# A mixture-of-experts stage whose fifth group of rows is halved and worked ahead of the fourth

## The reference

```
probs = softmax(x @ gate_w); w, sel = top_k(probs, 8); w = w / sum(w)
# each expert gets the rows (tokens) that chose it, at most C = 2048
g = xg @ w_gate[e]; u = xg @ w_up[e]
y = (silu(g) * u) @ w_down[e]
out = zeros.at[t_slot].add(w_slot[:, None] * y)
x = x + out
```

## Time and profile before

| | |
|---|---|
| median of 3 runs | 2238.33 us |
| the profiled execution | 2235.58 us |
| its span | 2233.8 us |
| mean granted TensorE clock over the span | 0.976 |
| TensorE matmul busy | 2041.8 us (91%) |
| VectorE / ScalarE / GpSimd busy | 1682.9 / 1149.9 / 1541.2 us |
| first transpose of the experts' stage | 1172.8 us |

### The profile page before, as it was taken

One profiled execution on the slowest core, in us unless ns is written; L12 is line 12 of the kernel. 1 busy time (PEld: TensorE's weight loads), 2 busy tenths in 40 slices (PEclk: granted clock), 3 DMA queues, 4 the chain that ended last, 5 costly groups with the idle time before them and its releaser, 6 DMA issues. The chain is left out here.

```text
span 2233.8 us, 67151 instructions
## 1 busy us (share of the span) xinstructions
PE 2041.8 (91%) x22647; PEld 1497.9 (67%) x22712; DVE 1682.9 (75%) x3294; ACT 1149.9 (51%) x2826; POOL 1541.2 (69%) x1776
## 2 busy tenths in 40 slices
PE   1899999999999999999509999999999999999997
PEld 1576667666666676666306777777777777777775
DVE  6688999999999999997426677676776677666664
ACT  3355555565555556555314455555555555555553
POOL 7336667666766666666667777777777777777774
PEclk9999999999999999999859999999999999999998
DMA  3101100110111001001016888887788878987875
GB/s 104 39 26 40 39 28 28 38 34 28 33 38 33 28 33 38 33 24 45 21 34 154 174 181 164 187 181 174 168 173 180 184 175 169 186 185 161 180 158 87
DMA packets 141452, 222.72 MB, mean 100 GB/s; under 512 B 32944, under 2 KB 65840, under 8 KB 141360
## 3 DMA queue, kind: packets, MB, share of 16 engines
q0 software_dynamic: 74752, 144.02, 32.8%
q1 hardware_dynamic: 62000, 69.24, 10.1%
q10 hardware_dynamic: 4608, 8.39, 1.0%
HBM read 136.34 MB, written 96.73 MB: 104 GB/s over the span
## 5 line engine op out<-in xcount | busy, mean ns | idle before, releaser
L2151 POOL DMA_INDIRECT out_dram<-y,m_add x300 | 499.1, 1664 | 173.8 <-POOLq L2159 116.8
L2277 PE MATMUL ps<-xh,wh 128*128 128x256 f16 x1752 | 399.9, 273 | 6.9 <-PEq L2289 6.9
L2278 PE MATMUL ps<-xh,wl 128*128 128x256 f16 x1752 | 399.9, 273 | 0.0
L2143 POOL DMA_INDIRECT xg<-z_scratch,slot_t x292 | 295.3, 1011 | 96.8 <-issue 86.2
L630 POOL DMA_INDIRECT slot_scratch<-pair,slots x256 | 277.5, 1084 | 68.8 <-issue 47.6
L2354 ACT ACTIVATE y<-ps,wts_now 128x512 f32<-128x512 f32 x294 | 185.4, 682 | 141.3 <-ACTq L2353 141.2
L2282 PE MATMUL ps<-xl,wh 128*128 128x256 f16 x1752 | 239.6, 273 | 0.0
L2428 DVE SCALAR_TENSOR_TENSOR hx<-ps,s 64x256 f16<-64x256 f32 x146 | 62.2, 426 | 219.3 <-DVEq L2451 218.6
L2277 PEld LDWEIGHTS ps<-xh,wh 128*128 128x128 f16 x1752 | 171.7, 98 | 48.7 <-issue 15.4
L2370 ACT ACTIVATE xh<-ps 128x512 f16<-128x512 f32 x146 | 87.2, 597 | 224.4 <-ACTq L2369 224.4
L2278 PEld LDWEIGHTS ps<-xh,wl 128*128 128x128 f16 x1752 | 171.8, 98 | 33.7 <-issue 0.3
(11 more groups left out here) (341 smaller groups left out, 5108.9 us busy)
## 6 DMA issues: line engine op xcount, KB each, us to landing
wst<-in_L_ffn_w_gate_dram SPq DMA_DIRECT2D x32, 384.0 KB
wst<-in_L_ffn_w_up_dram SPq DMA_DIRECT2D x32, 384.0 KB
xt<-in_x_dram SPq DMA_DIRECT2D x32, 256.0 KB
ct<-in_ctx_dram SPq DMA_DIRECT2D x32, 256.0 KB, 2.6
out_dram<-x SPq DMA_DIRECT2D x32, 256.0 KB, 2.1
z_scratch<-zn ACTq DMA_DIRECT2D x32, 256.0 KB
wdst<-in_L_ffn_w_down_dram SPq DMA_DIRECT2D x32, 256.0 KB
out_dram<-y,m_add POOLq DMA_INDIRECT x300, 5.2
```

The lines of the kernel that those rows point to most:

```text
L2143: pool.indirect_dma_start(out=xg[b][:, h, :], out_offset=None, in_=z_d[:, :], in_offset=bass.IndirectOffsetOnAxis(ap=rows(h), axis=0)).the ...
L2151: pool.indirect_dma_start(out=acc_d[:, :], out_offset=bass.IndirectOffsetOnAxis(ap=m_add[:, k, h:h + 1], axis=0), in_=y[:, k, h, :], in_of ...
L2277: pe.matmul(ps[:, dst, 0:GROUP], wh[:, j, k, c0:c0 + P], xh[:, k, :], start=(k == 0), stop=False)
L2278: pe.matmul(ps[:, dst, 0:GROUP], wl[:, j, k, c0:c0 + P], xh[:, k, :], start=False, stop=False)
```

## The change

Rows 1024 to 1151 of an expert become a half group of one part (128 rows), in buffer 4, on all engines. It is worked after group 2 and ahead of group 3 (rows 768 to 1023). If an expert has more than 1152 rows, rows 1152 to 1279 follow behind group 3 as a group of their own with 256 row slots, whose second part is not used: its row numbers are set to spare ones that lie outside the output (`spare_rows`, `note_first`). Group 5 and later ones follow as before. Group 2 has no branch any more. ScalarE's loop is written out. The counts of landed scatters are kept for each part of a y buffer instead of for each buffer.

GpSimd's order for an expert with more than 1024 rows is now: gather group 2; scatter the last group of the expert before; gather the half group; wait for the scatters of earlier experts; scatter group 0; gather group 3; scatter group 1; gather group 0 of the next expert; scatter group 2; gather group 1 of the next expert; scatter the half group; and with more than 1152 rows: gather the rows from 1152 on; scatter group 3; and with more than 1280: gather group 5; scatter the group of the rows from 1152 on.

The diff, cut to its core:

```diff
@@ constants, GpSimd @@
+                    pool.iota(spare_rows[:, :].bitcast(mybir.dt.int32), pattern=[[P, 1]], base=TOK, channel_multiplier=1).then_inc(pool_step, 1)
@@ block2 @@
+            HALF_FROM = 4 * GROUP
+            HALF_TO = HALF_FROM + P
@@ GpSimd @@
+                def add_half(k):
+                    pool.reg_add(n_added[k][0], n_added[k][0], 16)
+                    pool.wait_ge(wy_ready[0], 1)
+                    pool.sem_inc(wy_ready[0], -1)
+                    scatter(k, 0)
+                def gather_half(e):
+                    gather(4, lambda h: slot_t[:, e * (CAP // P) + HALF_FROM // P, 0:1], 1)
+                def gather_rest(e):
+                    gather(4, lambda h: slot_t[:, e * (CAP // P) + HALF_TO // P + h, 0:1])
                 def expert(e):
                     n = pool.value_load(counts[0:1, e:e + 1], min_val=1, max_val=CAP)
+                    more = e + 1 < ne
+                    gather_group(e, 2, 2)
+                    add_rows(2)
+                    with pool.If(n > HALF_FROM):
+                        gather_half(e)
+                    with pool.If(n <= HALF_FROM):
+                        with pool.If(n > 3 * GROUP):
+                            gather_group(e, 3, 3)
+                    earlier_experts_added()
+                    add_rows(1)
+                    if more:
+                        with pool.If(n <= HALF_FROM):
+                            gather_group(e + 1, 0, 0)
+                    with pool.If(n > HALF_FROM):
                         gather_group(e, 3, 3)
+                    add_rows(0)
+                    with pool.If(n <= HALF_FROM):
                         if more:
                             gather_group(e + 1, 1, 1)
+                        with pool.If(n > 3 * GROUP):
+                            add_rows(1)
+                    with pool.If(n > HALF_FROM):
+                        if more:
+                            gather_group(e + 1, 0, 0)
+                        add_rows(1)
+                        if more:
+                            gather_group(e + 1, 1, 1)
+                        add_half(0)
+                        with pool.If(n > HALF_TO):
+                            gather_rest(e)
+                            add_rows(1)
+                            with pool.If(n > USUAL * GROUP):
+                                gather_group(e, USUAL, 2)
+                                add_rows(0)
+                            for g in range(USUAL + 1, NGRP):
+                                with pool.If(n > g * GROUP):
+                                    gather_group(e, g, 3)
+                                    add_rows(1)
@@ TensorE: turn, down and gate_up take the number of parts @@
-                    def group(g, b):
-                        turn(b)
-                        down(j, b)
-                        gate_up(j)
-                    group(1, 1)
+                    def group(b, parts=2, parts_before=2):
+                        turn(b, parts)
+                        down(j, b, parts_before)
+                        gate_up(j, parts)
+                    group(1)
                     n = count_of(pe, e)
-                    written_out_groups(pe, n, group)
+                    group(2)
+                    with pe.If(n > HALF_FROM):
+                        group(4, 1)
+                        group(3, 2, 1)
+                    with pe.If(n <= HALF_FROM):
+                        with pe.If(n > 3 * GROUP):
+                            group(3)
+                    with pe.If(n > HALF_TO):
+                        group(4)
+                        with pe.If(n > USUAL * GROUP):
+                            group(2)
+                            with pe.Fori(USUAL + 1, NGRP) as g:
+                                with pe.If(n > g * GROUP):
+                                    group(3)
@@ ScalarE @@
+                def weigh_half(k):
+                    all_scattered(k)
+                    act.activation(m_add[:, k, :], rows_now[:, :], ACT.Copy)
+                    act.reg_add(n_added[k][0], n_added[k][0], 16)
+                    act.wait_ge(y_ps, 1)
+                    act.sem_inc(y_ps, -1)
+                    act.activation(y[:, k, 0, :], ps[:, 5, :], ACT.Copy, scale=wts_now[:, 0:1]).then_inc(act_step, 1)
...
+                def note_first(col):
+                    act.activation(rows_now[:, 0:1], slot_t[:, bass.ds(col, 1), 0], ACT.Copy)
+                    act.activation(rows_now[:, 1:2], spare_rows[:, :], ACT.Copy)
+                    act.activation(wts_now[:, 0:1], slot_t[:, bass.ds(col, 1), 1].bitcast(F32), ACT.Copy).then_inc(act_step, 1)
...
+                    group(c0 + 4, 0)
+                    with act.If(n > HALF_FROM):
+                        group(c0 + 8, 1, parts=1)
+                        group(c0 + 6, 0, weigh=weigh_half)
+                    with act.If(n <= HALF_FROM):
+                        with act.If(n > 3 * GROUP):
+                            group(c0 + 6, 1)
+                    with act.If(n > HALF_TO):
+                        group(c0 + 9, 1, note=note_first)
...
```

More of the change, by code:

```diff
@@ L2245, in turn @@
                             k = 2 * bank + n
-                            for h in range(2):
+                            for h in range(parts):
                                 c0 = n * GROUP + h * P
@@ L2249, in turn, with down @@
                         m.then_inc(signal, 1)
-                def down(j, b=None):
+                def down(j, b=None, parts=2):
                     pe.wait_ge(hx2_ready, 2)
                     pe.sem_inc(hx2_ready, -2)
-                    for h in range(2):
+                    for h in range(parts):
                         o, t = ps[:, 5 + h, :], slice(h * P, h * P + P)
@@ L2350, in weigh @@
                     act.activation(m_add[:, k, :], rows_now[:, :], ACT.Copy)
+                    for h in range(2):
+                        act.reg_add(n_added[k][h], n_added[k][h], 16)
                     for h in range(2):
@@ L2432, in gated, with group @@
                     dve.tensor_tensor(low, full, hi, ALU.subtract).then_inc(low_signal, 1)
-                def group(split=None, look=None):
+                def group(split=None, look=None, parts=2):
+                    t = slice(0, parts * P)
+                    rows = [ps[:, bank, :].rearrange("p (k t) -> p k t", k=2)[:, :, t] for bank in range(2)]
                     dve.wait_ge(rows_ps_dve, 1)
                     dve.sem_inc(rows_ps_dve, -1)
-                    dve.tensor_copy(xh[:, 2:4, :], ps[:, 1, :].rearrange("p (k t) -> p k t", k=2)).then_inc(xh_high_k_pe, 1)
+                    dve.tensor_copy(xh[:, 2:4, t], rows[1]).then_inc(xh_high_k_pe, 1)
                     dve.wait_ge(xh_low_k, 1)
@@ L2462, in expert @@
                     n = group((lambda: split_low_down(1 - j)) if more else None, lambda: count_of(dve, e))
-                    written_out_groups(dve, n, lambda g, b: group())
+                    group()
+                    with dve.If(n > HALF_FROM):
+                        group(parts=1)
+                        group()
+                    with dve.If(n <= HALF_FROM):
+                        with dve.If(n > 3 * GROUP):
+                            group()
+                    with dve.If(n > HALF_TO):
+                        group()
+                        with dve.If(n > USUAL * GROUP):
+                            group()
+                            with dve.Fori(USUAL + 1, NGRP) as g:
+                                with dve.If(n > g * GROUP):
+                                    group()
                 dve.memset(dl[I2:2 * I2, 0, 1, :], 0.0)
```

131 lines of the change are left out of this document (50 added, 81 removed).

## The result

| | before | after |
|---|---|---|
| median | 2237.36 us (4 runs, 2236.01 to 2238.59) | 2463.02 us (4 runs, 2461.26 to 2469.71) |
| span of the profiled execution | 2233.8 us | 2460.5 us |
| mean granted TensorE clock | 0.976 | 0.946 |

The ratio is 1.1019, between 1.1004 and 1.1034: 226 us slower. The forecast was 2308 us and its range ended at 2385. The sign was right. The case that came true is the rival that code is fetched again, at some 160 us instead of the 75 that I had put on it.

What follows compares the result with a forecast made beforehand. TensorE, busy 91% of the span, was taken to bound the kernel. Terms -83.5 + 60.0 + 22.1 + 33.5 + 22.5 + 13.2 + 2.2 = +70.0 us gave a 2308 us median; range 2264 to 2385.

Steps and rivals of the forecast that it cites:

- code is fetched again: Rival: TensorE's grown expert loop is no longer held, so jumps wait for code; about +75 us, 2383 us, chance 0.24.
- (a): On TensorE, twelve experts with 1025 to 1152 rows lose a full group of 6.96 us: -83.5 us.
- (b): On TensorE, all seventeen experts with more than 1024 rows gain a half group of 3.53 us: +60.0 us.
- (c): TensorE's waits around the half group, with ScalarE and VectorE late: 1.3 us in each of seventeen experts, +22.1 us.
- (d): Rows from 1152 on, gathered behind the half group's scatter, come late: TensorE waits 6.7 us in five experts, +33.5 us.
- (e): In three experts the further group's gather, queued behind the fourth group's scatters, comes late: 7.5 us each, +22.5 us.
- (f): TensorE's clock drops after eight long waits, losing 1.65 us each: +13.2 us.
- (g): Experts with a half group take two jumps on VectorE, delaying TensorE's next cast in six cases: +2.2 us.
- Only the half groups wait: Rival: late rows are hidden but waits around the half groups stand: +0.8 us, 2239 us, chance 0.04.
- The dropped groups decide: Rival: late rows arrive in time and half groups cost 3.53 us: -21 us, 2217 us, faster, chance 0.07.
- The half costs a full group's products: Rival: the half's 36 TensorE matmuls run at the old pace, bound by weight loads: +33 us, 2341 us, chance 0.05.

Runs made afterwards that it cites:

- e1: The changed kernel with the never-reached loop for groups 6 and 7 left out on TensorE alone: 2433.37 us, 1.048 times the kernel before.
- e3: The changed kernel with the loop for groups 6 and 7 left out on ScalarE and VectorE alone: 2531.17 us, 1.0901 times the kernel before.
- short form: The changed kernel without the loop for groups 6 and 7 on TensorE, ScalarE and VectorE; run as e2, e11 and e12: 1.0343, 1.0356, 1.0346.
- e2: The changed kernel with the loop for groups 6 and 7 left out on TensorE, ScalarE and VectorE: 2401.68 us, 1.0343 times the kernel before.
- e11: The same kernel as e2, run again on another chip: 2411.44 us, 1.0356 times the kernel before.
- e12: The same kernel as e2, run on the chip of the fourth set: 2405.59 us, 1.0346 times the kernel before.
- e5: e2 with GpSimd's gathers of the rows from 1152 on and of group 5 moved earlier: 2245.62 us, 1.0030 times the kernel before.
- fourth set: Runs on one chip, among them e12, e13, e15 and e9's kernel again; the kernel before takes 2322.57 us there.
- e9: e6 with group 5's rows gathered one step earlier and all 16 expert pairs inside the loop: 2354.92 us, 1.0111 times the kernel before.
- e6: e5 with groups 5 to 7 in one loop on three engines and ScalarE's row-number note behind the silus: 2245.08 us, 1.0042 times before.
- e15: The kernel before with one never-taken group per expert added on TensorE: 2453.89 us, 1.0572 times the kernel before.
- e13: The same kernel as e5, run on the chip of the fourth set: 2362.92 us, 1.0171 times the kernel before.

## Why the prediction was wrong, step by step

**The failed step is the rival "code is fetched again": its chance of 0.24 and its price of 30 x 2.5 = 75.** The sum put this term at nothing, on the ground that the loop stays held; I left the chance at 0.24 because nothing in the trace said where the limit is. The runs place it between 1,847 and 1,885 by my count, and the change went to 2,077. The price came from one row, 2.15 us at 1247.00, which is a jump in the loop's first passes. In the loop that is fetched in every pass, such waits come 34 times and last 3.4 us on average, 6.12 at the top of a pair and 11 after an expert with three groups, where more code is jumped over. So their number, 34 for my 30, was right, and their length was not. To the 111 us of waits comes the lower clock behind half of them, 2.1 us in the example above, and what the rival left out altogether: ScalarE's and VectorE's code is fetched again too, for another 32 us. In all, e1 to e3 give 129 + 32 = 161 us, where the rival had 75; with it the range ended at 2385, and the measured 2463 lies outside. The kernel after (1.1050) less its short form (1.034 to 1.036, on other chips) gives 0.07 x 2237 = 156.

**The forecast's own sum held step by step; that its total fits so well is in part luck.** Without the fetches the change costs 1.034, 1.036 and 1.035 on three chips (e2, e11, e12); the sum said 2308 / 2238.3 = 1.031. But those are the slower chips, on which versions with a half group lose about one and a half per cent more. On the faster chip that form did not run: e5 stands 9 us above the kernel before there, and moving the gathers was worth 43 us in the fourth set. By these two, as an estimate, the short form would stand some 52 us above it, against 70 in the sum, and the fetches would be some 174 of the 226 us. By its steps:

- (a), (b): casts 151. An expert whose full fifth group became a half takes 32.68 us in e5 against 34.81 before: -2.13. The steps gave -6.96 + 3.53 + 1.3 = -2.13.
- (c): 1.3 us put down, in the places named. In expert 12, half to next transposes is 4.70, down projection after 1.61 (0.74 late), gate products 1.56 after that (0.48 late), and the half's own down projection 0.10 late: 1.32.
- (d): 33.5 put down, the five waits are 8.88, 5.95, 6.56, 6.25 and 6.76: 34.4. They wait for the gather that stands behind the half group's scatter, as the two timelines of expert 17 show.
- (e): 22.5 put down, the three waits are 6.66, 7.21 and 6.55: 20.4. e5 takes (d) away whole and most of (e), by order alone.
- (f): 13.2 put down for eight waits. In the 5 us behind each of them the clock is at 0.50 to 0.72, which is 16.5 us lost in all. It falls behind 17 of the waits for code too, with 32 us lost in the same 5 us.
- (g): too small to be told apart here.

**Where the 226 us are.** Groups -23.5, half groups' waits +22, late rows +55, waits of the transposes for code +111: 165. Of the other 61, matmuls at the lower clock make some 50, by the granted clock in the 5 us behind each new wait, 26 stretches. TensorE's busy time of the stage agrees in size: 1068.20 us against 1029.89, with 23.5 us less of work, makes 62. The few us that are left have no row of their own, and ScalarE's and VectorE's fetches, 32 us by e1 and e2, could not be told apart in this sum.

**The other rivals.** *Only the half groups wait* comes out when both other causes are taken away: it gave 0.8 us on top of before, and e5 has 9.4 on its chip, much of it the rest of the waits for rows. *The dropped groups decide* fell, since (c) alone uses the 21 us up. *The half costs a full group's products* fell: the half's gate products take the pace of 128 columns, or 4.70 could not be.

**Open.** Why three of the four chips run the kernel before 4% slower, and the versions with a half group slower still, and whether e9 would beat the kernel before on the other chip. Whether the limit is the body's size alone or also where the body begins; a body was not shifted without being changed in size.

## What to carry to other kernels

Count the instructions of a loop body on each engine before a branch is added to it, the ones that never run too: 232 never-run instructions made this kernel 5.7% slower. Read the packets of the instruction queues against the number of passes, since a queue that is silent through the loop is a property that the change can lose. And when a piece of work is put ahead of another, follow its transfers on the queue that issues them: the late rows cost 55 us in waits, and moving their gathers took nearly all of these away.

## What the runs showed of the hardware that was not expected

- The step is sharp. A body of 1,847 TensorE instructions (e6) fetches 41 packets in all, one of 1,885 (e15, another kernel) fetches 151 and loses 131 us; 2,000 and 2,115 fetch about as much (134, 160).
- It has a second form on ScalarE and VectorE: with bodies of 430 and 384 the other queue carries 135 packets, with 374 and 334 it carries 62, and 32 us go.
- Waits for code hurt twice: behind 6.12 us without an instruction, TensorE took 5.11 us for what takes 3.03 at the full clock; the granted clock of the first 5 us is 0.58.
- One program takes 2236 us on one chip and 2322 to 2329 on three others, some 54 us of it ahead of the experts' stage, and the versions with a half group lose about one and a half per cent more on those (e5 1.0030, the same kernel as e13 1.0171).
